# Gathered expert rows turned by 32x32 blocks on VectorE, with h in block order in DRAM

## What is computed

```python
h = einsum('bsi,boi->bso', x, cond_weight[adapter_ids])          # 8 x 256 x 1024
probs = softmax(h @ gate_w.T); topk_vals, topk_idx = top_k(probs, 2); topk_vals /= sum(topk_vals)
g, u = split(einsum('th,eih->eti', h, w_gate_up))                # 16 experts, 2 x 256 inner columns
moe = einsum('eth,te->th', einsum('eti,ehi->eth', silu(g) * u, w_down), combine)
gs, us = split(h @ shared_w_gate_up.T)                           # 2 x 1024 inner columns
out = x + moe + (silu(gs) * us) @ shared_w_down.T
```

## Time and profile before

| | us |
|---|---|
| median of three runs | 1123.12 |
| profiled execution | 1124.23 |
| its span | 1122.7 |
| PE busy | 1107.8 (99%) |
| VectorE busy | 567.1 (51%) |
| ScalarE busy | 475.7 (42%) |
| GpSimd busy | 164.9 (15%) |
| DMA | 247.45 MB, mean 220 GB/s |

### The profile page before, as it was taken

The page is one execution under the profiler, slowest core; times in us unless marked ns, Lnnn a source line. Parts: engine busy times, 40 slices in busy tenths (PEclk is TensorE's granted clock), DMA queues, the critical chain, the costliest instruction groups (busy, mean ns, idle before and its releaser), DMA issues.

```text
span 1122.7 us, 16952 instructions
## 1 busy us (share of the span) xinstructions
PE 1107.8 (99%) x5250; PEld 916.8 (82%) x5251; DVE 567.1 (51%) x638; ACT 475.7 (42%) x602; POOL 164.9 (15%) x246
## 2 busy tenths in 40 slices
PE   8999999999999999999999999999999999999998
PEld 7788888888887888888888888778888888888887
DVE  5555555435854446565544644444462445425453
ACT  6556565432223456665655655533240323213220
POOL 1112121000011011111111111042003210032140
PEclk9999999999999999999999999999999999999999
DMA  9787776622255567877786787364255642564345
GB/s 350 286 325 265 283 287 223 228 75 76 75 225 206 206 225 273 287 279 281 271 327 224 286 317 294 130 246 169 75 225 209 212 179 108 211 235 156 112 154 220
DMA packets 40931, 247.45 MB, mean 220 GB/s; under 512 B 4994, under 2 KB 5122, under 8 KB 30594
## 3 DMA queue, kind: packets, MB, share of 16 engines
q1 hardware_dynamic: 14530, 154.15, 36.5%
q0 software_dynamic: 19456, 69.22, 17.9%
q10 hardware_dynamic: 6912, 23.66, 5.6%
HBM read 201.39 MB, written 49.81 MB: 224 GB/s over the span
## 4 chain that ended last, share of the span: by engine, by line
PE 97%; issue 1%; ACT 1%; DMA 1%; DVE 0%; ACTq 0%; DVEq 0%
PE bank L510 30%; PE bank L512 30%; PE bank L511 30%; PE bank L678 3%; PE bank L531 1%; PE bank L523 1%; PE bank L711 1%; DMA x_raw_sb<-xT 1%; DVE w_split_sb L1051 0%; ACT hT_hi L792 0%; ACT w_split_sb L792 0%; PE bank L645 0%; ACT y_out L792 0%; PE bank L540 0%; ACTq L781 0%
## 5 line engine op out<-in xcount | busy, mean ns | idle before, releaser
L1051 DVE TENSOR_TENSOR w_split_sb<-raw,w_split_sb 128x2048 fp32r<-128x2048 f32 (+3 forms) x152 | 259.0, 1728 | 93.3 <-ACT w_split_sb L792 92.1
L792 ACT ACTIVATE w_split_sb<-raw 128x2048 fp32r<-128x2048 f32 (+3 forms) x152 | 218.1, 1462 | 95.3 <-PE bank L512 85.4
L510 PE MATMUL bank<-hT_hi,w_split_sb 128*128 128x512 f32 x512 | 199.8, 390 | 0.9 <-ACT y_out L792 0.9
L512 PE MATMUL bank<-hT_hi,w_split_sb 128*128 128x512 f32 x512 | 199.2, 389 | 0.0
L511 PE MATMUL bank<-hT_lo,w_split_sb 128*128 128x512 f32 x512 | 199.2, 389 | 0.0
L510 PE MATMUL bank<-w_split_sb,tile_hT 128*128 (+1 forms) x312 | 125.6, 402 | 2.8 <-issue 2.7
L512 PE MATMUL bank<-w_split_sb,tile_hT 128*128 (+1 forms) x312 | 122.4, 392 | 0.0
L511 PE MATMUL bank<-w_split_sb,tile_hT 128*128 (+1 forms) x312 | 122.2, 392 | 0.0
L510 PEld LDWEIGHTS bank<-hT_hi,w_split_sb 128*128 128x128 f32 x512 | 96.1, 188 | 21.0 <-issue 1.3
L512 PEld LDWEIGHTS bank<-hT_hi,w_split_sb 128*128 128x128 f32 x512 | 96.1, 188 | 20.1
L511 PEld LDWEIGHTS bank<-hT_lo,w_split_sb 128*128 128x128 f32 x512 | 96.1, 188 | 19.9
(11 more groups left out here) (148 smaller groups left out, 1527.2 us busy)
## 6 DMA issues: line engine op xcount, KB each, us to landing
raw<-sh_gu_w SPq DMA_DIRECT2D x16, 2048.0 KB, 9.1
raw<-exp_gu_w SPq DMA_DIRECT2D x16, 2048.0 KB
raw<-cond_w SPq DMA_DIRECT2D x14, 2048.0 KB, 8.4
y_dram<-y_out ACTq DMA_DIRECT2D x39, 512.0 KB
raw<-sh_down_w SPq DMA_DIRECT2D x8, 2048.0 KB, 7.7
raw<-exp_down_w SPq DMA_DIRECT2D x16, 1024.0 KB, 7.5
h_dram<-h_row POOLq DMA_DIRECT2D x32, 256.0 KB, 6.0
x_raw_sb<-xT SPq DMA_DIRECT2D x7, 1024.0 KB, 11.0
```

The lines of the kernel that those rows point to most:

```text
L510: nc.tensor.matmul(dst, lhs[0], rhs[0], start=first, stop=False)
L512: return nc.tensor.matmul(dst, lhs[1], rhs[0], start=False, stop=last)
L792: return nc.scalar.activation(dst, src, ACT.Copy)
L1051: return nc.vector.tensor_tensor(dst, src, hi.bitcast(F32), ALU.subtract)
```

## The change

h is stored once, in block order: a row of `h_dram` holds its 1024 features as four blocks j of 256, block j being features 128k + 32j + c for k of 0 to 7 and c of 0 to 31. ACT writes it to `h_blk` beside `h_row`, in all four quarters, and POOL stores 512 KB at a time; PE waits for that copy (`hb_ev`) ahead of the bank's next use. `hT_dram`, `hT_raw` and their stores go.

A tile's gather becomes four indirect DMAs of 128 pieces of 1 KB: partition 32j + t of `h_in` gets, at place i, block j of the token in slot 32i + t. A transpose of 32x32 blocks on DVE (`tile_turn`) then makes `tile_f32`, features in partitions and tokens in columns; ACT and DVE split it from SBUF. The row numbers need the token's index in other partitions: DVE spreads the identity, PE multiplies it with the indices (`spread_tokens`), DVE scales and adds (`route_rows`). `transpose_tile` on PE goes.

In `tile_step`, the turn and both halves of the split of tile s+1 stand behind those of `e_aT` and ahead of the weight splits, Silu and product. `tile_f32` lies in the half of `raw[1]` that the down weights leave free, so the first shared weights into `raw[1]` wait for the last tile.

For the shared quarters SP loads `h_dram` in block order by four DMAs into `q_blk`, and DVE turns it in four parts into `q_f32`. The first of these loads moves from behind all expert weights to behind those of expert 1, and its turns stand behind step 2 (`tile_step(2)`); those of later quarters stand behind the second and third unit of the down part, and the lo halves of `hT` follow later than before.

```diff
-    hT_dram = nc.dram_tensor("hT_dram", [QUARTERS - 1, P, KT, QTOK], F32).ap()
...
+    tile_f32 = [at(f"tile_f32{i}", [P, KT, P], F32, 24 + 4 * i) for i in range(2)]
...
-    hT_raw = [at(f"hT_raw{i}", [P, 4, P], F32, 192 + 2 * i) for i in range(4)]
-    h_in = [at(f"h_in{i}", [P, HID], F32, 192 + 4 * i) for i in range(2)]
+    h_blk = at("h_blk", [P, 2, BLOCKS, KT, 32], F32, 192)
+    q_blk = at("q_blk", [P, QTOK // 32, HID // BLOCKS], F32, 144)
+    q_f32 = at("q_f32", [P, KT, QTOK], F32, 176)
+    h_in = [at(f"h_in{i}", [P, BLOCKS, HID // BLOCKS], F32, 192 + 4 * i) for i in range(2)]
...
-            sp.wait_ge(routed, 2)
+            sp.wait_ge(routed, 1)
...
+            h_quarters = h_dram.rearrange("(q i t) (j c) -> q j t i c", q=QUARTERS, t=32, j=BLOCKS)
+            def load_hT(qq):
+                for j in range(BLOCKS):
+                    sp.dma_start(q_blk[32 * j:32 * (j + 1), :, :],
+                                 h_quarters[bass.ds(qq, 1), j, :, :, :].rearrange("o t i c -> (o t) i c")).then_inc(hT_in[j], 16)
+            loads_and_fill(0)
+            for m in range(QM):
+                sp.wait_ge(rows_out[m], 16)
+            sp.wait_ge(gu_mm, 3)
+            load_hT(0)
+            with sp.Fori(1, FILL) as f:
+                loads_and_fill(f)
...
+            sp.wait_ge(et_lo, 2 * run + 3)
...
+            def cond_stores(q):
+                for b2 in range(2):
+                    for m in range(2):
+                        wait(hb_ev, UPQ * q + 4 * b2 + 2 + m + 3)
+                        pool.dma_start(h_dram[bass.ds(q * QTOK + b2 * SEQ + m * P, P), :],
+                                       h_blk[:, m, :, :, :].rearrange("p j k c -> p (j k c)")).then_inc(h_store[m], 16)
+            with pool.Fori(0, QUARTERS) as q:
...
+            h_blocks = h_dram.rearrange("t (j c) -> (t j) c", j=BLOCKS)
             def gather_h(s, par):
-                wait(et_mm, 2 * s + 2)
-                nc.gpsimd.tensor_copy(idx_h[par][:, :], small["tok_idx"][:, bass.ds(s, 1)]).then_inc(idx_ready, 1)
+                wait(e_turned, s + 1)
+                nc.gpsimd.tensor_copy(idx_h[par][:, :], small["row_idx"][:, bass.ds(s, 1), :].rearrange("p o i -> p (o i)")).then_inc(idx_ready, 1)
                 wait(idx_ready, s + 1)
-                nc.gpsimd.indirect_dma_start(
-                    out=h_in[par][:, :], out_offset=None, in_=h_dram,
-                    in_offset=bass.IndirectOffsetOnAxis(ap=idx_h[par][:, 0:1], axis=0)).then_inc(h_gather[par], 16)
+                for i in range(BLOCKS):
+                    nc.gpsimd.indirect_dma_start(
+                        out=h_in[par][:, i, :], out_offset=None, in_=h_blocks,
+                        in_offset=bass.IndirectOffsetOnAxis(ap=idx_h[par][:, i:i + 1], axis=0)).then_inc(h_gather[par], 16)
...
+                            pe.wait_ge(hb_ev, UPQ * q + u + 1)
...
-            def transpose_tile(s, par, count, first_bank=4):
-                pe.wait_ge(h_gather[par], 16 * count)
-                for hf in range(2):
-                    pe.wait_ge(et_lo, 2 * s + hf + 1)
-                    for i in range(4):
-                        k = 4 * hf + i
-                        last = nc.tensor.transpose(bank[first_bank + hf][:, i * P:(i + 1) * P], h_in[par][:, k * P:(k + 1) * P], ident[:, :])
-                    last.then_inc(et_mm, 1)
...
+            def spread_tokens(m):
+                if m == 1:
+                    pe.wait_ge(rt_tokf, 1)
+                    for i in range(BLOCKS):
+                        last = nc.tensor.matmul(bank[7][:, 128 + i * TPAD:128 + (i + 1) * TPAD], rt["spread"][:, i, :],
+                                                rt["tok_f"][:, :], start=True, stop=True)
+                    last.then_inc(rt_spread, 1)
...
-            def tile_step(s, par, nxt_count):
+            def tile_step(s, par):
                 (_, e1_before, odd_before), (_, e1, odd) = load_meta(mybir.EngineType.PE, s - 1, 2)
                 gate_up_tile(s, par, e1, odd)
-                transpose_tile(s + 1, 1 - par, nxt_count)
                 down_tile(s - 1, 1 - par, e1_before, odd_before)
...
                 act.wait_ge(t_mm, UPQ * q + u + 3)
-                if not last:
-                    if u >= 4:
-                        act.wait_ge(hT_store[u - 4], 16 * q + 16)
-                    elif not first:
-                        act.wait_ge(hT_store[u + 4], 16 * q)
-                    copy(hT_raw[u % 4][:, :, :], bank[4 + m][:, :].rearrange("p (k t) -> p k t", k=4)).then_inc(t_raw, 1)
...
                     copy(h_row[:, m, :], bank[m][:, :]).then_inc(h_ev, 1)
+                    if n == 0 and (not first or b2):
+                        act.wait_ge(h_store[m], 16 * (2 * q + b2))
+                    copy(h_blk[:, m, :, 4 * n:4 * n + 4, :].rearrange("p j k c -> p k j c"),
+                         bank[m][:, :].rearrange("p (k j c) -> p k j c", k=4, j=BLOCKS)).then_inc(hb_ev, 1)
...
+            for m in range(2):
+                act.wait_ge(h_store[m], 16 * QUARTERS * 2)
...
-            def tile_hi(s, dst, first_bank=4):
-                for hf in range(2):
-                    act.wait_ge(et_mm, 2 * s + hf + 5)
-                    copy(dst[:, 0, 4 * hf:4 * hf + 4, :].rearrange("p k t -> p (k t)"), bank[first_bank + hf][:, :]).then_inc(et_hi, 1)
+            def tile_hi(s, par, dst):
+                act.wait_ge(e_turned, s + 3)
+                copy(dst[:, 0, :, :], tile_f32[par][:, :, :]).then_inc(et_hi, 1)
...
                 act_hi(s - 1, 1 - par)
+                if not last:
+                    act.wait_ge(gu_mm, s + 2)
+                    tile_hi(s + 1, 1 - par, tile_hT[1 - par])
...
                 silu_tile(s, par)
-                tile_hi(s + 1, tile_hT[1 - par])
...
+                step(nc.vector.tensor_copy(rt["spread"][:, :, :].rearrange("p i (j t) -> p i j t", t=32),
+                                           ident[:, :].rearrange("p (i t) -> p i t", t=32).unsqueeze(2).to_broadcast([P, BLOCKS, BLOCKS, 32])))
...
+            def route_rows():
+                dve.wait_ge(rt_spread, 1)
+                nc.vector.tensor_scalar(small["row_idx"][:, :, :].rearrange("p t i -> p i t"),
+                                        bank[7][:, 128:128 + BLOCKS * TPAD].rearrange("p (i t) -> p i t", i=BLOCKS),
+                                        float(BLOCKS), small["block_of"][:, 0:1], ALU.mult, ALU.add).then_inc(rows_known, 1)
...
+            def tile_turn(par, count):
+                dve.wait_ge(h_gather[par], 16 * BLOCKS * count)
+                nc.vector.transpose(tile_f32[par][:, :, :].rearrange("p k (i t) -> p i k t", t=32),
+                                    h_in[par][:, :, :].rearrange("p i (k c) -> p i k c", c=32)).then_inc(e_turned, 1)
+            def tile_lo(s, par, dst):
+                dve.wait_ge(et_hi, s + 1)
+                lo(dst[:, 1, :, :], tile_f32[par][:, :, :], dst[:, 0, :, :]).then_inc(et_lo, 1)
...
+            def hT_turn_parts(landed, parts):
+                for j in range(BLOCKS):
+                    dve.wait_ge(hT_in[j], landed)
+                for i in parts:
+                    nc.vector.transpose(q_f32[:, 2 * i:2 * i + 2, :].rearrange("p k (i t) -> p i k t", t=32),
+                                        q_blk[:, :, 64 * i:64 * (i + 1)].rearrange("p i (k c) -> p i k c", c=32)).then_inc(hT_turned, 1)
...
                 act_lo(s - 1, 1 - par)
+                if not last:
+                    tile_turn(1 - par, count)
+                    tile_lo(s + 1, 1 - par, tile_hT[1 - par])
...
                 mul_tile(s, par)
-                tile_lo(s + 1, tile_hT[1 - par])
...
+            tile_step(1, 1, 2)
+            tile_step(2, 0, 2)
+            hT_turn_parts(16, range(4))
...
+            turns_after = {(0, 1): (0, 1), (0, 2): (2, 3)}
+            parts_after = {(1, 0): (0, 1), (1, 1): (2, 3)}
```

164 lines of the change are left out of this document (64 added, 100 removed).

## The result

The changed kernel takes 1174.58 us, the median of four executions (1170.45 to 1176.80), against 1122.93 of the kernel before on the same chip: a ratio of 1.0458 (95% interval 1.0440 to 1.0476). The change makes the kernel 4.6% slower. The profiled execution took 1176.8 us with a span of 1174.9.

What follows compares the result with a forecast made beforehand. PE (TensorE) was taken to bound the kernel: 1124.2 - 34.8 (transposes) + 34.0 (late products) + 0.95 + 1.5 + 0.9 + 0.5 (ends, new matmuls) = 1127.3, given as 1126 us against the median; range 1108 to 1154.

Steps and rivals of the forecast that it cites:

- part 1: Tile transposes taken off PE: eight per tile at 0.87 us over 40 tiles, -34.8 us if nothing is late.
- Part 2: DVE and ACT work per tile: copies and differences nearly nothing in sum, the new DVE turn 1.24 us.
- Part 3: Expert steps: turn, copy and difference ahead of the product make it late where weights are split, stalling PE, +34.0 us.
- e: Time from PE's transposes of e_act to ACT's next e_aT copy; 2.0 to 2.4 us, on even steps 2.6 to 4.
- the four classes: Stalls in expert steps by down or gate-up weights and even or odd step, 34.7 us in sum.
- Slope: Change of total time per 0.1 us of T, DVE's turn time per tile: 2.1 us over some 21 stalled steps.
- rival (c): DVE's turn takes its upper bound, 2.3 us, stalling every step with weights: 1154 us; chance 0.10.
- Part 4: Ends of the expert stage: +0.95 us at the first tiles, +1.5 and +0.9 in the last steps, +0.5 for new matmuls.
- Part 5: h in DRAM, its stores, copies and shared-quarter loads and turns: nil, up to 6 us if loads land late.
- Part 6: Tile gathers as four indirect DMAs on POOL, 5.3 us per tile, wanted 17 us later: nil, up to 5 us.
- rival (d): Gathers land over 17 us after their start and hold the product too; ten of 5 us, 1175 us; chance 0.04.
- Rival (b): Expert-stage stalls half as large, from shrinking ACT issue or a turn near 0.78 us: 1109 us; chance 0.26.

Runs made afterwards that it cites:

- run 3: Against run 1, DVE turns the tile after next behind the product, and tile 2's gather goes between POOL's row stores: 1118.37 us, ratio 0.9959.
- run 7: Against run 1, DVE's turn of the tiles is left out, so the values are wrong: 1137.80 us, ratio 1.0123.
- run 8: Against run 1, DVE turns every tile twice, the second turn waiting for the first: 1209.61 us, ratio 1.0765.
- run 5: The edits of run 2 and run 3 together, against run 1: 1104.31 us, ratio 0.9831.
- run 10: Against run 1, only tile 2's gather moves, between the second and third store of rows on POOL: 1163.31 us, ratio 1.0366.
- run 2: Against run 1, PE reads three tiles' entries ahead of its wait for the product, for two steps at a time: 1150.76 us, ratio 1.0247.
- run 1: The changed kernel with only a mask on the expert's number added, which changes no value: 1174.32 us, ratio 1.0454.

## Why the prediction was wrong, point by point

The sign of the likeliest case was right (slower), its size was not: 1126 was forecast, 1108 to 1154 the range, 1174.6 is the time.

- **Bounds now, part 1.** Right: L678 is gone and the work of a step is 8.42 us for 9.32, 0.9 per step where 0.87 was taken.
- **Part 2.** Right. The turn takes 1235 ns (1.24 was taken) and the difference behind it 1225 (1.22):

```profile
L1321 DVE STREAM_TRANSPOSE tile_f<-h_in 128x1024 f32<-128x1024 f32 x39 | 48.2, 1235 | 8.3 <-DMA h_in<-h_dram,idx_h 8.2
```

 The estimate from the Trainium skill (VectorE: DVE Perf Modes, The three transpose paths), one element a cycle, agrees as well.
- **Part 3, the product's time.** Right: in the step at 472.49 `e` is 3.58 and the product ends at 10.66, `e` + 7.08, with `e` + 7.1 worked out. PE's waits for the product are 34.2 us in all, and the four classes gave 34.7, but that is luck. 5.7 of them are step 0, which was written off; steps 1 to 34 hold 27. And the classes are off one by one:

| us of wait, steps 1 to 34 | worked out | measured |
|---|---|---|
| down weights, even steps | 17.7 | 13.3 |
| down weights, odd steps | 8.5 | 0 |
| gate-up weights, even steps | 5.2 | 12.5 |
| gate-up weights, odd steps | 2.6 | 1.3 |

 In the odd steps with down weights the product ends at 9.3 to 9.5 us (in one at 10.5), later than the 8.45 at which it was due, and PE does not wait: reads and slow clock have made it as late itself. Aside from step 0, ten even steps have waits of 2.0 to 2.7 us, all others 1.2 or less.
- **Part 3, what a stall costs.** This is the step that failed. The sum adds the stall alone, and takes for granted that PE goes on at once and at full pace. It does neither. 28.1 us of reads and 27.6 of slow clock, 52.6 more than in the kernel before, stand against a miss of 48.6 (the stalls and the start came out somewhat smaller than worked out). The pattern was in the trace of before. I read the earlier trace rows, 1.25 us of issue behind the first product, as a thing of step 0, and did not ask what PE's sequencer does there; nor did I look at what followed such a gap: in the timeline of the kernel before, the matmuls behind it (366.23 on) start 0.43 us apart for two microseconds. The chain of the kernel before has one more, in the conditioning, followed by matmuls 0.43 us apart:

```profile
33.74 0.44 PE bank L523 x4
34.18 2.77 issue
...
38.03 0.43 PE bank L510
38.46 0.43 PE bank L511
```

 With the two terms the working would have been: for each of ten even steps with a wait of 2 us, 0.8 to 2.1 us of reads and 1.2 to 2.9 us of slow clock in the step behind it.
- **Part 3, the cover.** The product was taken to be due 8.45 us after the last transposes. Run 3 shows steps where it ends 0.8 to 0.9 us before PE's transposes and gate_up is still 0.8 to 0.9 us late. Due is about a microsecond earlier, since PE has to get through the wait in time to read ahead of its work.
- **Slope.** "A tenth of a microsecond of T is worth 2.1 us", and 2 to 3 in rival (c); runs 7 and 8 measure 2.9 and 2.8. The slope was near, the level was 48 us off. That a slope fits is no evidence for a level; run 8, too, came out where this slope and not my later theory put it.
- **Part 4.** At tile 0 the changed kernel is 4.3 us ahead, where -0.3 was worked out; the gap of 2.77 us and its slow matmuls in the conditioning, shown above, are not in the new trace, and they are about the difference. The four spread matmuls came as eight on the trace and took 0.83 us for 0.5. The tail was worked out as -0.2 (1.5 and 0.9 against three times -0.87) and is +2.5: the last step but one took 11.64 us for 11.7, but the last, taken as unchanged at 9.55, took 11.27, with 2.1 us of wait and 0.7 of reads. So the forecast's parts were -0.3, +3.6 (34.0 less 35 x 0.87) and -0.2, and the measured ones are -4.3, +53.9 and +2.5.
- **Part 5.** The traces show no wait of PE in the conditioning or shared stages that was not there before. Nil was right for this kernel. It had little to spare: the four turns behind `tile_step(2)` make down wait 2.0 and 3.6 us for `e_aT` in runs 3 and 5, where PE is earlier and the next tile's gather stands ahead of them.
- **Part 6 and rival (d).** Wrong in one place. "Wanted 17 us later" holds in the loop, and there no gather is late; for tile 2 the gather stands behind four stores in POOL's queue, and this one gather costs 11 us (run 10). It stood there in the kernel before, too (first gather at 361.03), but there PE wanted the rows at 372.63, and now DVE stands ready for them at 362.3. I asked when gathers start in the loop, and not what the earlier need meets in POOL's queue. That the time is the 1175 of rival (d) is luck: it had ten late gathers of 5 us, and there is one. The mean of an indirect DMA was taken over at 966 ns and is 1191, also without effect on the end.
- **Rival (b).** That stalls would be half as large: no; ACT's issue ahead of the `e_aT` copy is 65.1 us over 28 waits, 67.9 before.
- **What would show it.** The list named PE's idle time ahead of L711 and the length of the steps without weights. It had no line on the clock or on the gap behind L711, so the list could confirm the mechanism and miss half the loss.

What stays open: why the reads take 0.8 to 0.9 us in some odd steps (3, 5, 7, 19, 21) and 1.9 to 2.1 in others (9 to 17, each behind a step with down weights and a wait of over 2 us). In run 2 the loop's branch and its If moved ahead of the wait along with the reads. Odd steps have neither, so the reads alone can cost this much, but no run tells what branch and If add in the even ones (1.5 us in steps 6, 24 and 34). The move of the reads ahead also brought 17 us of new waits where 8 were expected; which product became later by it was not followed up.

## What to carry to other kernels

When an input of the bounding engine becomes late, price three things: the wait, what its sequencer does between that wait and its next work (register reads, branches, which had been free while the engine ran behind), and the clock of the matmuls that follow. Put new work of a helper engine behind what the bounding engine waits for next, not ahead of it, and judge an edit that takes work off the bounding engine by the time of its next input, not by the work: here 31.5 us of PE's work went, and putting it back made the kernel faster. And when the loss is on record, first take a gap that the profile calls "issue" at its word: moving PE's reads was worth 24 us.

## What the runs showed of the hardware

- **The clock falls after short idle times.** In run 2, where a gap is the wait alone, twelve of the steps 1 to 34 had waits of 2.0 to 2.7 us, and seven of them were followed by 1.4 to 1.6 us of slow clock; of the eight waits of 0.8 to 1.65 us none was. In steps 0 to 34 of the changed kernel twelve of fourteen gaps (wait and reads together) of over 2.0 us were. What decides between them is not shown; this one, of 3.2 us in step 36, was not followed by slow matmuls, where a gap of 3.6 us in the same place of run 1 was:

```profile
752.02 0.38 PE L713 MATMUL bank<-ident,e_act 128*128 128x128 f32 x2
755.35 0.50 PE L514 MATMUL bank<-w_split_sb,tile_hT 128*128 x1 [2.95 <-issue]
755.68 0.40 PE L515 MATMUL bank<-w_split_sb,tile_hT 128*128 x1
```

 The level is 1.2 GHz by the spacing of the matmuls, 0.43 us for 0.23. The Trainium skill (TensorE: Matmul & The Clock Gate, The HAM clock gate) has the two levels 1.2 and 2.4 GHz; the spacings agree with them.
- **Reads behind a semaphore wait.** PE's reading of two tiles' entries adds 0.8 to 2.1 us between a wait and the next matmul when nothing covers it (odd steps of the changed kernel). In the kernel before, whose product is early, steps 1 to 34 show nothing of it: gate_up starts 0.13 to 0.14 us behind the transposes in each.
- **An f32 turn by 32x32 blocks** of 1024 columns, SBUF to SBUF, takes 1233 to 1245 ns in all 39 instances.
- **Some gathers take twice as long beside DVE.** The first of the four indirect DMAs of a tile takes 1.9 us where the other three take 0.95, in the step shown above while DVE works on the difference of the tile (479.19 to 480.41), which has two inputs in SBUF:

```profile
479.33 1.93 POOL L457 DMA_INDIRECT h_in<-h_dram,idx_h  x1 [0.81 <-POOL idx_h L454]
481.56 0.95 POOL L457 DMA_INDIRECT h_in<-h_dram,idx_h  x1 [0.30 <-issue]
```

 The Trainium skill (SBUF — State Buffer, Who interferes with whom) has DVE instructions with two SBUF inputs contend with GpSimd instructions that read SBUF. The rows agree in part only. The first indirect DMA starts beside the tile's difference in 35 of 39 tiles, and takes 1.9 us in all 35. The second starts beside a difference of weights, whose two inputs are in SBUF as well (480.45 to 482.82 in the step above), in 30 tiles, and takes 0.95 us in all but one of them. What sets the two apart is not shown. A turn holds none of them up: the nine indirect DMAs that start beside one (two here, seven in run 3) take 0.94 to 1.01 us. In this kernel the microsecond is covered.
